# Relative values through the transposes' ring, values two steps behind the scores, and another order of three DMAs on SyncE

## What is computed

```python
def proj(W):                                   # 16 heads of width 16
    return (x @ W.T).reshape(b, s, H, HD).transpose(0, 2, 1, 3)
Q, K, V = (proj(Wq), proj(Wk), proj(Wv))
idx = clip(r[None, :] - r[:, None], -256, 256) + 256
scores = (einsum('bhqd,bhkd->bhqk', Q, K) + einsum('bhqd,qkd->bhqk', Q, pek[idx])) / HD ** 0.5
scores = where(causal, scores, -inf)
attn = softmax(scores, axis=-1)
out = einsum('bhqk,bhkd->bhqd', attn, V) + einsum('bhqk,qkd->bhqd', attn, pev[idx])
```

## Time and profile before

| what | value |
|---|---|
| median of 3 runs | 5536.34 us |
| the profiled execution | 5535.59 us |
| its span, first to last instruction | 5533.9 us |
| granted clock of TensorE, mean of the span | 0.990 |
| PE busy | 5134.9 us (93%) |
| DVE busy | 3774.5 us (68%) |
| ACT busy | 3425.3 us (62%) |
| POOL busy | 1831.3 us (33%) |
| DMA: moved, rate over the span | 1418.07 MB, 256 GB/s |

### The profile page before, as it was taken

How to read it: one execution, slowest core, us unless ns; L and a number is a source line. 1 busy time by engine, 2 the same in 40 slices (tenths; PEclk the granted TensorE clock), 3 DMA queues, 4 the chain that set the end, 5 groups by cost and what they waited for, 6 DMA issues and landing times. The chain is left out here.

```text
span 5533.9 us, 143122 instructions
## 1 busy us (share of the span) xinstructions
PE 5134.9 (93%) x49460; PEld 3347.5 (60%) x49460; DVE 3774.5 (68%) x8777; ACT 3425.3 (62%) x7512; POOL 1831.3 (33%) x2516
## 2 busy tenths in 40 slices
PE   9986999999999999999999999999999799999999
PEld 5554666666666666666666666666666455665665
DVE  5555777777777777777777777777777455555554
ACT  4445888878778887887877878778787211111111
POOL 3443333333333333333333333333333011111111
PEclk9997999999999999999999999999999899999999
DMA  7888999999999999999999999999999311111110
GB/s 223 254 252 264 329 323 324 332 316 323 321 324 324 325 323 321 324 328 325 322 325 327 322 321 327 316 323 327 324 322 304 99 61 56 50 61 61 61 55 32
DMA packets 654368, 1418.07 MB, mean 256 GB/s; under 512 B 64072, under 2 KB 362544, under 8 KB 641456
## 3 DMA queue, kind: packets, MB, share of 16 engines
q1 hardware_dynamic: 653744, 1409.89, 77.5%
HBM read 737.46 MB, written 672.14 MB: 255 GB/s over the span
## 5 line engine op out<-in xcount | busy, mean ns | idle before, releaser
L809 ACT ACTIVATE a_prob<-a_neg_s,a_neg_max 128x384 f32<-128x384 f32 (+1 forms) x1792 | 1081.1, 603 | 209.1 <-DVE a_neg_max L858 193.2
L524 DVE COPY a_p_t<-a_t_ps 128x512 f32<-128x512 f32 (+3 forms) x1536 | 952.5, 620 | 24.8 <-PE a_t_ps L773 23.9
L773 PE MATMUL a_t_ps<-a_ident,a_prob 128*128 128x128 f32 x5120 | 924.5, 280 | 31.5 <-DVE a_p_t L524 20.4
L858 DVE CUSTOM_DVE_ANT_1 a_neg_s<-a_s_ps,a_bias,a_far_neg 128x384 f32<-128x384 f32 x1280 | 791.0, 618 | 237.6 <-DVE a_far_neg L852 237.6
L706 PE MATMUL a_s_ps<-a_k,a_q 96*128 96x512 bf16 (+3 forms) x3072 | 852.7, 332 | 107.2 <-ACT a_far L813 105.1
L852 DVE TENSOR_REDUCE a_far_neg<-a_s_ps 128x1 f32<-128x640 f32 (+4 forms) x1280 | 708.8, 554 | 312.0 <-PE a_s_ps L706 178.5
L816 ACT ACTIVATE a_b_out<-a_t_ps 128x512 f32<-128x512 f32 (+1 forms) x1024 | 587.4, 574 | 384.4 <-PE a_t_ps L716 364.6
L734 PE MATMUL a_o_ps<-a_p_t,a_v 128*32 128x128 f32 x18432 | 782.0, 279 | 7.8 <-ACT a_o_t L821 0.2
L813 ACT ACTIVATE a_far<-a_s_ps,a_neg_max 128x640 f32<-128x640 f32 (+4 forms) x1280 | 730.6, 571 | 0.0
L816 ACT ACTIVATE a_p_t<-a_t_ps 128x512 f32<-128x512 f32 (+3 forms) x1536 | 672.8, 438 | 71.0 <-PE a_t_ps L773 53.4
L773 PE MATMUL a_t_ps<-a_ident,a_far 128*128 128x128 f32 x3840 | 662.5, 278 | 55.5 <-DVE a_p_t L524 52.2
(11 more groups left out here) (99 smaller groups left out, 6678.4 us busy)
## 6 DMA issues: line engine op xcount, KB each, us to landing
a_bias<-bias_scr SPq DMA_DIRECT2D x448, 576.0 KB, 7.8
prob_scr<-a_prob SPq DMA_DIRECT2D x448, 576.0 KB, 6.5
bias_scr<-a_b_out SPq DMA_DIRECT2D x448, 512.0 KB, 7.1
a_band<-prob_scr SPq DMA_DIRECT2D x448, 512.0 KB, 5.6
qk_scr<-p_parts SPq DMA_DIRECT2D x256, 192.0 KB, 3.4
v_scr<-p_v_out SPq DMA_DIRECT2D x256, 128.0 KB, 2.2
a_v<-v_scr SPq DMA_DIRECT2D x64, 512.0 KB, 8.9
attn_scr<-a_o_t SPq DMA_DIRECT2D x512, 64.0 KB, 7.4
```

The costliest lines, as they stand in the source:

```text
L524: copy(p_t[par][:, head, blocks[0] * P:(blocks[-1] + 1) * P], bank[:, 0:len(blocks) * P]) \
L773: mm = pe.transpose(bank[:, n * P:(n + 1) * P], prob_block(r, kk, head, b), ident[:, :])
L809: e = act.activation(near_prob(r, k, u, near(qb)), neg_s[:, u % 2, 0:w].rearrange("p (b c) -> p b c", c=P), ACT.Exp, bias=neg_max[:, u:u + ...
L858: dve.tensor_tensor_reduce(by_block(neg_s[:, u % 2, 0:w]), by_block(s_ps[:, u % 2, lo:lo + w]), near_bias(r, k, u, near(qb)), -1.0, begin, ...
```

## The change

Relative values. `relative` no longer adds to `o_ps`. It is a job "rel" of the plan, last in slot 0, takes a bank of the ring (its first 128 columns) and starts its own sum there. DVE adds that bank to `o_t` in place (`read_out`), and counts `o_sum`; the next user of the bank and SP's store wait for it. `values` ends its own sum, and ACT copies `o_ps` to `o_t` at the end of slot 3 of the same step, after the last part of `values`, and no longer in slot 0 after `relative`. `o_t` has 4 buffers in place of 2.

Lags. `P_LAG` is 5 in place of 7, and `values` works on tile k - 2 in place of k - 3, in the same slots. With the lag of 5, slot 0 has head 3 of tile k - 2, and slots 1 to 3 have heads 0 to 2 of tile k - 1; with 7 they were heads 1 to 3 of tile k - 2 and head 0 of tile k - 1. An even step has 8 jobs, an odd step 14. Bands and `relative` keep their places (tiles k - 3 and k - 4).

SP. In a step the bias read comes first, then the probabilities' write, then the band read. Their waits are the same.

```diff
+    OUT = 4
-        o_t = sb("a_o_t", [P, 2, P])
+        o_t = sb("a_o_t", [P, OUT, P])
+        o_sum = sem("a_o_sum")
-        P_LAG = 7
+        P_LAG = 5
         BAND_SLOTS = ((2, 3), (3, 3))
-        VALUE_SLOTS = ((1, 3), (2, 3), (3, 3))
+        VALUE_SLOTS = ((1, 2), (2, 2), (3, 2))
...
+                if u == REL_SLOT[0] and ok(k - REL_SLOT[1]) and k >= 0:
+                    jobs.append(("rel", u, k - REL_SLOT[1], 0, None))
...
+            if kind == "rel":
+                eng.wait_ge(o_sum, TILES * r + kk + 1)
...
+                if kind == "rel" and name == "dve":
+                    eng.wait_ge(o_mm, TILES * r + kk + 1)
+                    eng.wait_ge(o_evac, TILES * r + kk + 1)
+                    eng.tensor_tensor(o_t[:, kk % OUT], o_t[:, kk % OUT], bank[:, 0:P], ALU.add).then_inc(o_sum, 1)
...
-                    if k >= 0 and ok(k - 2):      # SP: band read of tile k - 2
-                        ...
                     if k + 2 >= 0 and ok(k + 2):  # SP: bias read of tile k + 2
                         ...
+                    if k >= 0 and ok(k - 1):      # SP: probabilities' write of tile k - 1 (was ahead of the bias read)
+                        ...
+                    if k >= 0 and ok(k - 2):      # SP: band read of tile k - 2 (was the first)
+                        ...
...
-                        sp.wait_ge(o_evac, T - 3)
+                        sp.wait_ge(o_sum, T - 3)
...
-                                       p_t[par][:, h, j * P:(j + 1) * P], start=(j == 0), stop=False)
+                                       p_t[par][:, h, j * P:(j + 1) * P], start=(j == 0), stop=(j == qb))
...
-            def relative(r, k):
+            def relative(r, k, bank):
...
-                        mm = pe.matmul(o_ps[h * VW:(h + 1) * VW, 0:P], pv[:, n], band_t[:, par, h, n * P:(n + 1) * P],
-                                       start=False, stop=(n == 1))
+                        mm = pe.matmul(bank[h * VW:(h + 1) * VW, 0:P], pv[:, n], band_t[:, par, h, n * P:(n + 1) * P],
+                                       start=(n == n_first), stop=(n == 1))
...
+                            elif kind == "rel":
+                                relative(r, kk, bank)
...
-                        if u == REL_SLOT[0] and ok(k - 4) and k >= 0:
-                            act.wait_ge(o_mm, T - 3)
+                        if u == VALUE_SLOTS[-1][0] and ok(k - 2) and k >= 0:
+                            act.wait_ge(pv_mm, T - 1)
                             if ok(k - 6):
                                 act.wait_ge(stored[k % 2], pair(r, k - 6))
-                            act.activation(o_t[:, k % 2], o_ps[:, 0:P], ACT.Copy).then_inc(o_evac, 1)
+                            act.activation(o_t[:, (k - 2) % OUT], o_ps[:, 0:P], ACT.Copy).then_inc(o_evac, 1)
```

More of the change, by code:

```diff
@@ L495, in wait_evac @@
             kind, _, kk, i, head = job
-            if kind == "band":
+            if kind == "rel":
+                eng.wait_ge(o_sum, TILES * r + kk + 1)
+            elif kind == "band":
                 eng.wait_ge(r_evac[i], TILES * r + kk + 1)
@@ L580, in body @@
                     T = TILES * r + k
-                    if k >= 0 and ok(k - 2):
[L583 to L595, removed]
                     if k + 2 >= 0 and ok(k + 2):
@@ L606, in body @@
                         sp.dma_start(bias[:, par, B_RAW:B_RAW + n], src).then_inc(b_loaded[par], 16)
+                    if k >= 0 and ok(k - 1):
+                        sp.wait_ge(wide_ready, T)
+                        n = run_of(q_block(k - 1)) + P
+                        rows = prob_scr[(k - 1) % 4, 0:P * n].rearrange("(q c) -> q c", c=n)
+                        sp.dma_start(rows, wide_prob(r, k - 1)).then_inc(p_saved[(k - 1) % 4], 16)
+                    if k >= 0 and ok(k - 2):
+                        par = k % 2
+                        if ok(k - 4):
+                            sp.wait_ge(r_mm, 2 * (T - 4) + 2)
+                        sp.wait_ge(set_ready, SET)
+                        sp.wait_ge(p_saved[(k - 2) % 4], quad(r, k - 2))
+                        n = run_of(q_block(k - 2))
+                        src = bass.AP(prob_scr.tensor, (k - 2) % 4 * P * WIDE + 1, [[n + P + 1, P], [1, n]])
+                        sp.dma_start(moved_band(k - 2), src).then_inc(p_loaded[par], 16)
                     if k % 2 and ok(k + LEAD):
@@ L624, in body @@
                         qb, g = q_block(k - 4), ((k - 4) % TILES) // QB
-                        sp.wait_ge(o_evac, T - 3)
+                        sp.wait_ge(o_sum, T - 3)
                         row = attn[r_prev if k < 4 else r]
-                        sp.dma_start(row[g, :, qb * P:(qb + 1) * P], o_t[:, par]).then_inc(stored[par], 16)
+                        sp.dma_start(row[g, :, qb * P:(qb + 1) * P], o_t[:, (k - 4) % OUT]).then_inc(stored[par], 16)
             written_out(n_iter, body)
@@ L743, in relative @@
                     pe.wait_ge(r_evac[i], TILES * r + k + 1)
-                for n in range(first_j(q_block(k)) // P, 2):
+                n_first = first_j(q_block(k)) // P
+                for n in range(n_first, 2):
                     for h in range(GRP):
-                        mm = pe.matmul(o_ps[h * VW:(h + 1) * VW, 0:P], pv[:, n], band_t[:, par, h, n * P:(n + 1) * P],
-                                       start=False, stop=(n == 1))
+                        mm = pe.matmul(bank[h * VW:(h + 1) * VW, 0:P], pv[:, n], band_t[:, par, h, n * P:(n + 1) * P],
+                                       start=(n == n_first), stop=(n == 1))
                 mm.then_inc(o_mm, 1)
@@ L783, in body @@
                                 mm.then_inc(r_mm, 1)
-                        if u == REL_SLOT[0] and ok(k - 4) and k >= 0:
-                            relative(r, k - 4)
                         for part, (at, back) in enumerate(VALUE_SLOTS[:-1]):
```

## The result

The changed kernel takes 5576.31 us (median of 4 runs, 5575.2 to 5581.7), the kernel before beside it 5536.53: a ratio of 1.0073, interval 1.0056 to 1.0091. It is slower by 40 us where 122 us less were forecast.

What follows compares the result with a forecast made beforehand. Even steps were taken as paced by DVE, odd ones by PE with ring hand-overs. Terms -1.8 - 0.9 + 0.8 = -1.9 us a pattern, times 64 = -122 us, gave 5414 us (5415 on the median's scale), likely range 5360 to 5460.

Steps and rivals of the forecast that it cites:

- (4): Ring in odd steps: 14 jobs for 11, a same-slot bank wait happens twice; +0.8 us a pattern.
- (1): DVE in even steps, which it paces: -0.60 us each, -2.4 a pattern, three quarters of it taken, -1.8.
- (2): DVE and ACT in odd steps: DVE's +1.0 us is hidden; step 1 might cost 0.2 at most.
- (3): Bias read first on SP: earlier masks save half of DVE's 1.79 us wait, -0.9 a pattern; band read stays covered.
- same-slot wait: In odd steps, the band's transposes wait for ACT's bias copy, 0.27 us each; to happen twice a step, not once.
- (5): Shorter lag: `values` needs head 3's copies one slot after their transposes, not three; adds nothing.
- D: Rival: slower, odd steps held by the ring with 14 jobs over three banks; 5592 us, chance 0.14.
- C: Rival: no change, odd steps take what even ones give; 5530 us, chance 0.08.
- A: Rival: transfers take over, bias read pushes the write by 1.8 us and the band read; 5472 us, chance 0.18.
- D's turning point: Odd step length beyond which D loses: 7.73 + 0.45 us, a bank's time of 1.75 us.
- The bank's time of 1.37 us: Time a bank is held in a slot with short maxima, used against D: c = 1.45, 6.8 us an odd step.

Runs made afterwards that it cites:

- e2: Changed kernel with SyncE's old order (band read, probabilities' write, bias read); 5567.1 us.
- e3: Kernel before with only the relative values' part (bank of the ring, VectorE's sum, output copy in slot 3), old lags and SyncE order; 5617.2 us.
- e14: e7 with the relative values taken out of the ring, into other columns of the values' bank, still added by VectorE; 5559.4 us.
- e7: e3 with the ring's banks counted through from step to step instead of restarting at 0; 5603.8 us.
- e20: e8 with the relative values out of the ring, beside the values as in e14; 5522.3 us, ratio to before 0.9979.
- e4: Changed kernel with the lags of before (7 slots, values 3 steps behind); 5644.3 us.
- e19: Kernel before with one 128x512 copy more on VectorE in slot 1 of each even step; 5669.5 us.
- e8: e2 with the ring's banks counted through from step to step; 5563.4 us.
- e10: e7 without VectorE's added sum, so the output lacks the relative values; 5586.2 us.
- e17: e8 with four transposes more on PE in slot 1 of each odd step; 5671.3 us.
- e16: e8 with one 128x512 copy more on VectorE in slot 1 of each odd step; 5645.0 us.
- e9: Kernel before with SyncE's bias read first, band read and probabilities' write in their old order behind it; 5543.1 us.
- e1: Kernel before with only SyncE's new order (bias read, probabilities' write, band read); 5584.2 us.

## Why the prediction was wrong

The sum was -1.9 us a pattern; measured is +0.6 (44 us over the 5532.5 us of the later runs, by 64, is +0.7). As a ledger of the runs, from before to the changed kernel, in us a pattern (us in brackets):

| part | forecast | measured |
|---|---|---|
| lags: VectorE's relief, -0.80 x 4 by three quarters, and (4)'s +0.8 | -1.6 | -0.8 (-50, e2 less e3) |
| sum and output copy: +0.20 x 4 by three quarters | +0.6 | +0.4 (+26, e14) |
| place in the ring | not costed | +0.7 (+44, e7 less e14) |
| count restarted in each step | not costed | +0.2 (+13, e3 less e7) |
| SyncE's order | -0.9 | +0.1 (+9, changed less e2) |

The steps lead from one kernel to the other, so that they add up to about +42 us is no check. The parts depend on each other: the lags gave 37 to 68 us by what stood beside them (e14 to e20, e4 to the changed kernel), the order cost 9 to 52. Three steps of the prediction failed, each by 0.7 to 1 us a pattern: the lags' cover in odd steps, the order, and a place in the ring put at nothing.

- **The ground of (1) holds.** VectorE paced the even steps (e19), and its relief came back there: the copies alone were put at 3.2 us a pattern, three quarters of it to come, and 2.1 came (e7 to e8). In the changed kernel the even steps are 0.59 a pattern shorter, 0.15 a step for the forecast's 0.4. The sum was sized rightly as an instruction and cost 18 us or less (e10). The trace of before had a nearer row for it than the one taken, an add of the same form over 512 columns in the feed-forward (L1125, 0.688 us, as long as a copy of 512 columns).
- **(2) failed: "Hidden, as long as the copies come in time".** With the long copies the odd steps took 1.6 us a pattern more (e7 to e8), where at most 0.2 was allowed for. In them PE's time counts nearly in full (e17) and VectorE's by half (e16). Comparing busy time with the step's length was the mistake: the shares said 5.6 of 7.8, and half of what VectorE got in addition came out as time. This turns the copies' -2.4 into -0.5 to -0.8 (e7 to e8 by steps, e3 to e2 by times); (4)'s +0.8 for four jobs in two slots is in it.
- **(3) failed in its sign.** The wait for the mask went, and the even steps gained 0.34 us a pattern (e9) of the 0.9 that was taken. The price was on the other side: the band, called covered "with 2 us in hand", came late in e1 because its read stood behind the write's wait for POOL (812.4 us on SP). (3) said that the write "may wait for POOL" and gave it no price. With the short lags little of it is left (+9), which the prediction didn't foresee either, and which no run explains.
- **(4) left out a term.** The same-slot wait came twice as often, as forecast. But the relative values' own place, in slot 0, was put at nothing without a reason: it costs +44 us with the lags of before and about 41 with the short ones (e8 less e20), in odd steps with the long ones. The seams add 13 with the long lags and 4 or less with the short ones.
- **(5) held** as far as it was seen: no wait for copies ahead of the values stands out in the changed kernel's list.
- **Rivals.** D (slower, odd steps held by the ring, chance 0.14) has the side that came, at 5576 for its 5592, but the size is luck: D made 14 jobs in an odd step the price of the lags, and the lags gained; the place costs with 12 jobs as well (e7). C has the lags' mechanism (what even steps give, odd ones take). A's mechanism is small: with the bias read first and nothing else moved (e9), the write's median time to landing went from 6.5 to 7.0 us and the band's from 5.7 to 6.0, not by 1.8. D's turning point, 8.18 us for an odd step, was set against a gain of 0.45 an even step; the odd ones have a mean of 8.05 (32.2 / 4), and the even ones gave 0.15 to 0.27. The bank's time of 1.37 us, on which it was set aside, came from one light slot of the kernel before.

## What to carry to other kernels

Where an engine's busy share is below the step's length but it hands over through a short ring, its spare time is not cover: ask what a copy's delay does to the job three banks on, and test with one instruction added in that slot before work is moved there. In a short ring a place can cost more than the work done in it; try a short job in a free corner of another bank first. When a DMA issue is moved ahead of another on an in-order queue, look at what the one in front waits for, not only at how many bytes it moves.

## What the runs showed of the hardware

In one place of e1 a PE that waited 1.8 us for the band (busy 0.41 of 2.20 us) ran the next 4.3 us at a mean granted clock of 0.60, so mostly at 1.2 and not 2.4 GHz, and was back at 1.00 in the window behind it. The step was 3.5 us longer than the same step of the kernel before: there a late transfer cost its wait and about as much again. The Trainium skill, page "TensorE: Matmul & The Clock Gate", section "Part 1: The HAM clock gate", says that the throttled state is the default and activity releases it; these windows agree, with 0.60 behind the idle stretch and 1.00 after 4.3 us of work.

The second surprise is of size: 44 us for a place in the ring (e7 less e14), where the job's instruction on VectorE, 512 times 0.286 us busy, came out as 18 us of the kernel's time (e7 less e10).
